# Three edits to a joined kernel: order of the values in the local attention, transposes in pairs of 64 rows in the causal attention, and a diagonal term in pairs of 64 rows in the last attention

## The reference

```
layer 0, ffn branch: 6 x { local attention (16 heads of 64, windows of 32, each looks at
                           itself and the window before), then a gated feed-forward }
layer 2, attn branch: sim = (q k^T)/8 + slope_h * (j - i), masked to j <= i; softmax; @ v
                      (16 heads of 64)
layer 3, attn branch: logits = (q k^T)/sqrt(8) - alpha_h * |i - j|; softmax; @ v
                      (16 heads of 8, no mask)
```

## Time and profile before

| what | value |
|---|---|
| median of 3 runs | 4435.03 us (4434.4 to 4439.9) |
| the profiled execution, its own time | 4430.25 us |
| its span | 4428.5 us |
| TensorE (PE), weight loads (PEld) | 3915.2 us (88%), 2158.4 us (49%) |
| VectorE, ScalarE, GpSimd | 3103.5 (70%), 2556.6 (58%), 1247.7 us (28%) |
| granted clock of TensorE, mean | 0.926 |

### The profile page before, as it was taken

One profiled execution on the slowest core, in us unless ns is written; L12 is line 12 of the kernel. 1 busy time (PEld: TensorE's weight loads), 2 busy tenths in 40 slices (PEclk: granted clock), 3 DMA queues, 4 the chain that ended last, 5 costly groups with the idle time before them and its releaser, 6 DMA issues.

```text
span 4428.5 us, 113349 instructions
## 1 busy us (share of the span) xinstructions
PE 3915.2 (88%) x46366; PEld 2158.4 (49%) x46462; DVE 3103.5 (70%) x5185; ACT 2556.6 (58%) x3768; POOL 1247.7 (28%) x1082
## 2 busy tenths in 40 slices
PE   3789999999999999867778999999997599999997
PEld 1365555555555555535553555555553233333333
DVE  7788888888888888645414666666664677777772
ACT  5456666666666667552224555555553276767774
POOL 0366656655566566310000000000000011111220
PEclk7899999999999999965578999999998699999998
DMA  0222222222222222201000000000000300000000
GB/s 18 71 67 75 69 65 80 71 72 74 65 76 72 68 76 68 55 10 24 21 9 17 3 4 4 4 2 4 4 1 26 100 19 20 19 20 19 19 2 15
DMA packets 85355, 166.74 MB, mean 38 GB/s; under 512 B 23336, under 2 KB 37336, under 8 KB 83568
## 3 DMA queue, kind: packets, MB, share of 16 engines
q1 hardware_dynamic: 84816, 159.13, 13.8%
HBM read 40.60 MB, written 8.52 MB: 11 GB/s over the span
## 4 chain that ended last, share of the span: by engine, by line
PE 46%; issue 19%; POOL 15%; DVE 12%; ACT 5%; DMA 1%; SPq 1%; POOLq 0%; DVEq 0%; ACTq 0%
POOL arena L987 7%; POOL arena L991 6%; PE banks L1287 6%; PE banks L2237 5%; PE banks L1270 4%; PE banks L1258 4%; ACT arena L2373 2%; PE banks L522 2%; PE banks L2195 2%; PE banks L2211 2%; PE banks L1306 1%; DVE arena L861 1%; DVE arena L1438 1%; PE banks L2215 1%; PE banks L605 1%
## 5 line engine op out<-in xcount | busy, mean ns | idle before, releaser
L2447 DVE TENSOR_REDUCE arena<-banks 128x2 f32<-128x1024 f32 x512 | 614.2, 1223 | 248.6 <-PE banks L2202 140.4
L2373 ACT ACTIVATE arena<-banks 128x1024 f32<-128x1024 f32 x512 | 522.8, 1025 | 252.7 <-PE banks L2218 134.2
L987 POOL TENSOR_TENSOR arena<-arena 128x512 f32<-128x512 f32 x384 | 424.5, 1127 | 637.4 <-DVE arena L870 629.8
L991 POOL TENSOR_TENSOR arena<-arena 128x1024 f32<-128x1024 f32 x192 | 533.1, 2776 | 15.1
L1438 DVE CUSTOM_DVE_ANT_0 arena<-arena,banks 128x512 f32<-128x512 f32 (+3 forms) x640 | 361.9, 603 | 202.6 <-issue 201.3
L1381 ACT ACTIVATE arena<-banks 128x512 f32<-128x512 f32 (+3 forms) x320 | 170.2, 532 | 401.7 <-PE banks L1270 401.0
L522 PE MATMUL banks<-arena 128*128 128x512 f32 x768 | 366.7, 622 | 30.8 <-issue 15.0
L2237 PE MATMUL banks<-arena 128*32 128x256 f32 x4096 | 334.4, 393 | 14.2 <-issue 8.7
L1518 POOL COPY arena<-arena 128x512 f32<-128x512 f32 x32 | 19.6, 613 | 1123.5 <-DVE arena L1464 1123.5
L1373 ACT ACTIVATE arena<-arena 128x128 f32<-128x128 f32 (+15 forms) x256 | 328.6, 1285 | 11.3 <-DVE arena L1450 6.3
L1258 PE MATMUL banks<-arena 64*128 64x512 f32 (+3 forms) x1280 | 322.3, 581 | 5.1 <-issue 3.8
(11 more groups left out here) (433 smaller groups left out, 7384.3 us busy)
## 6 DMA issues: line engine op xcount, KB each, us to landing
arena<-arena SPq DMA_DIRECT2D x768, 64.0 KB
arena<-arena SPq DMA_DIRECT2D x96, 384.0 KB, 3.6
arena<-arena SPq DMA_DIRECT2D x96, 128.0 KB, 3.4
arena<-in_lf_wqkv SPq DMA_DIRECT2D x6, 1024.0 KB, 6.0
arena<-features_k SPq DMA_DIRECT2D x32, 128.0 KB
arena<-arena SPq DMA_DIRECT2D x8, 512.0 KB
arena<-features_q SPq DMA_DIRECT2D x16, 216.0 KB
arena<-in_lf_wqkv SPq DMA_DIRECT2D x6, 512.0 KB, 3.8
```

Source lines behind the costliest of these rows:

```text
L987: nc.gpsimd.tensor_tensor(r[:, :, e * H2:(e + 1) * H2], q[:, j, :, (1 - e) * H2:(2 - e) * H2], s[:, j, 1, e * H2:(e + 1) * H2].unsqueeze(1 ...
L991: nc.gpsimd.tensor_tensor(a, a, lf_rb, ALU.add).then_inc(S("lf_rot" + x), 1)
L2373: nc.scalar.activation(bi_PT[n % 4], PS[:, 2 * bi_slot("S", n):2 * bi_slot("S", n) + 2].rearrange("p a b -> p (a b)"), ACT.Exp).then_inc(S ...
L2447: nc.vector.tensor_reduce(bi_max[j % 2][:, t, :, c], PS[:, 2 * slot:2 * slot + 2], AX.X, ALU.max).then_inc(S("bi_mx"), 1)
```

## The change

It does three things. In the local attention, `values` is one call that does both parities before `project`. In the causal attention, each 128 x 128 transpose becomes two of 64 rows: the lower rows of both heads go to bank 4, the upper rows to bank 5; VectorE and ScalarE evict the same number of elements as before, now for both heads each; `turn` waits for both copies first, and carries markers (`sem_inc`). In the last attention, each matmul of the diagonal term is cut by its contraction into 64-row halves, with the slope of head 0 on rows 0 to 63 and of head 1 on rows 64 to 127, so that the two heads' matmuls stand side by side.

```diff
 (local attention)
-            def values(n, l, e):
-                vb = (lf_Vs if e == 0 else lf_V)[n % 4]
-                for p in range(8):
...
-                if e:
-                    m.then_inc(S("lf_pv"), 1)
+            def values(n, l):
+                for e, vb in enumerate((lf_Vs[n % 4], lf_V[n % 4])):
+                    for p in range(8):
...
+                m.then_inc(S("lf_pv"), 1)
 (its step)
                 if lf_live(s - 3, end):
-                    values(s - 3, l, 0)
+                    values(s - 3, l)
                 if lf_live(s - 4, end):
                     project(s - 4, l, end)
                 if ffn and j == 0:
                     var(c, l)
-                if lf_live(s - 3, end):
-                    values(s - 3, l, 1)
 (causal attention)
+                n = min(4, at_row(c, x) + 1 - 4 * b)
+                if i >= 1:
+                    pe.wait_ge(S("at_ptA"), l * 80 + i)
+                    pe.wait_ge(S("at_ptB"), l * 80 + i)
                 for h in range(2):
                     if b == 0:
                         pe.wait_ge(S("at_exp"), l * 64 + (2 * (2 * c + x) + h + 1))
-                    if i >= 1:
-                        pe.wait_ge(S("at_ptB" if h else "at_ptA"), l * 80 + i)
-                    for j in range(min(4, at_row(c, x) + 1 - 4 * b)):
-                        m = nc.tensor.transpose(PS[:, 4 + h, j * P:(j + 1) * P], ck(at_E[c % 2][x][h], 4 * b + j, P), ident)
-                    m.then_inc(S("at_trB" if h else "at_trA"), 1)
+                        pe.sem_inc(S("at_turning"), 1)
+                    elif h == 0:
+                        pe.sem_inc(S("at_turning"), 1)
+                    for j in range(n):
+                        k = h * n + j
+                        lower = nc.tensor.transpose(PS[:, 4, k * at_D:(k + 1) * at_D], ck(at_E[c % 2][x][h], 4 * b + j, P)[0:at_D], ident[0:at_D, 0:at_D])
+                        upper = nc.tensor.transpose(PS[:, 5, k * at_D:(k + 1) * at_D], ck(at_E[c % 2][x][h], 4 * b + j, P)[at_D:P], ident[at_D:P, at_D:P])
+                lower.then_inc(S("at_trA"), 1)
+                upper.then_inc(S("at_trB"), 1)
 (VectorE's copy; ScalarE's takes the upper 64 columns from bank 5 likewise)
-                nc.vector.tensor_copy(at_PT[x][0][:, 4 * b:4 * b + n, t % 2 * P:(t % 2 + 1) * P],
-                                      PS[:, 4, 0:n * P].rearrange("p (a b) -> p a b", b=P)).then_inc(S("at_ptA"), 1)
+                nc.vector.tensor_copy(at_PT[x][:, :, 4 * b:4 * b + n, t % 2 * P:t % 2 * P + at_D],
+                                      PS[:, 4, 0:n * P].rearrange("p (h a b) -> p h a b", h=2, b=at_D)).then_inc(S("at_ptA"), 1)
 (last attention; scores likewise)
-                    for h in range(2):
-                        for x in range(3):
-                            m = nc.tensor.matmul(PS[:, 2 * slot + h, t * P:n], ck(bi_aI[p], 2 * x + h, P), bi_trib[:, 0:P], start=False, stop=x == 2)
+                    for y in range(6):
+                        for h in range(2):
+                            m = nc.tensor.matmul(PS[:, 2 * slot + h, t * P:n], ck(bi_aI[p], y, P)[rows(h)], ck(bi_trib, y % 2, P)[rows(h)], start=False, stop=y == 5)
 (VectorE, once)
+            for h in range(2):
+                r = slice(64 * h, 64 * h + 64)
+                st(nc.vector.tensor_copy(bi_slope[r, :, 8:11], bi_slope[r, :, 0:6].rearrange("p a (x h) -> p a x h", h=2)[:, :, :, h]))
 (GpSimd, for each pair of heads)
-                for x in range(6):
-                    m = nc.gpsimd.tensor_tensor(ck(bi_aI[p], x, P), ident, bi_a[p][:, x:x + 1].broadcast_to([P, P]), ALU.mult)
+                for y in range(6):
+                    m = nc.gpsimd.tensor_tensor(ck(bi_aI[p], y, P), ck(bi_tri, 4 + y % 2, P), bi_a[p][:, 8 + y // 2:9 + y // 2].broadcast_to([P, P]), ALU.mult)
```

More of the change, by code:

```diff
@@ L1166, in program @@
         at_E = [[[arena.f32(n) for _ in range(2)] for n in (T // 2, T)] for _ in range(2)]
-        at_PT = [[arena.f32_3(n, 2 * P) for _ in range(2)] for n in (NB // 2, NB)]
+        at_PT = [arena.f32(2 * n * 2 * P).rearrange("p (h k q) -> p h k q", h=2, k=n) for n in (NB // 2, NB)]
         at_mx = [arena.f32_3(2, 4) for _ in range(2)]
@@ L2033, in program @@
         bi_cut = arena.bf16(bi_H)
[L2034 to L2037, removed]
+        bi_slope = arena.f32_3(8, 11)
+        bi_a = [arena.f32(11) for _ in range(2)]
+        bi_tri = arena.f32(6 * P)
+        bi_trib = arena.bf16(4 * P)
         bi_aI = [arena.bf16(6 * P) for _ in range(2)]
@@ L2212, in scores @@
                 if k // 4 == G:
-                    for h in range(2):
-                        for x in range(3):
-                            m = nc.tensor.matmul(PS[:, 2 * slot + h, n:n + P], ck(bi_aI[p], 2 * x + h, P), bi_trib[:, P:2 * P], start=False, stop=x == 2)
+                    for y in range(6):
+                        for h in range(2):
+                            m = nc.tensor.matmul(PS[:, 2 * slot + h, n:n + P], ck(bi_aI[p], y, P)[rows(h)], ck(bi_trib, 2 + y % 2, P)[rows(h)], start=False, stop=y == 5)
                 if n:
@@ L2336, in bi_act @@
             nc.scalar.activation(bi_idb, ident, ACT.Copy).then_inc(S("bi_idb"), 1)
-            nc.scalar.activation(bi_trib, bi_tri, ACT.Copy).then_inc(S("bi_idb"), 1)
+            nc.scalar.activation(bi_trib, bi_tri[:, 0:4 * P], ACT.Copy).then_inc(S("bi_idb"), 1)
             for c in range(NCH):
@@ L2738, in layout @@
     p = np.arange(P)
-    o["at3_tri"] = np.concatenate([-2 * np.maximum(p[None] - p[:, None], 0), -2 * np.maximum(p[:, None] - p[None], 0)], 1).astype(np.float32)
+    half = [p % 64 + 64 * f for f in range(2)]
+    o["at3_tri"] = np.concatenate([-2 * np.maximum(p[None] - x[:, None], 0) for x in half] + [-2 * np.maximum(x[:, None] - p[None], 0) for x in half]
+                                  + [p[None] == x[:, None] for x in half], 1).astype(np.float32)
     off = (p[:, None, None] + 128 * np.arange(4) - 512 * np.array([[1], [0]]))[:, :, None, :, None] * np.array([-1, 1])[None, None, :, None, None]
```

17 lines of the change are left out of this document (8 added, 9 removed).

## The result

The changed kernel takes 4365.3 us (median of four runs, 4359.6 to 4377.1) against 4434.7 for the kernel before on the same chip: ratio 0.9847, 95% interval 0.9823 to 0.9871. That is 69 us less where 128 were forecast, and 5 us above the top of the range given (4360). The profiled execution has a span of 4366.3 us, 62 less than before.

What follows compares the result with a forecast made beforehand. TensorE was taken to set the time in the causal and last attention, until VectorE is met. Terms -80 - 44 + 2 - 6 = -128 took 4430.25 to 4302, as a median 4307 us; range 4272 to 4360.

Steps and rivals of the forecast that it cites:

- Rivals B: Weight loads don't go under matmuls of their own rows, so a pair takes 0.114 us: 4374 us; chance 0.08.
- C: Causal transposes: the two halves don't run at once, each costing what a whole one does: 4596 us; chance 0.03.
- part 1: Causal attention's transposes as 64-row pairs: TensorE's sequence 130 us shorter, of which -80 us is kept; ends -125 and +209.
- the forecast's 0.5 and 0.6: Causal attention: TensorE's wait for copies, some 0.5 us in an odd pass and 0.6 in an even pass's last two units.
- the unit with the addition: Causal odd pass: after VectorE's addition L1477 the turn waits for two logits, a copy and the addition, 2.6 us, mostly covered.
- rival A: Causal attention: VectorE or ScalarE takes the gain; only even passes gain, 42 us instead of 80, so 4345; chance 0.13.
- Part 2: Last attention's diagonal matmuls as 64-row pairs: 472 changes of rows at 0.1 us go, -44 us; ends -50 and +88.
- Part 3: Local attention with both parities' values before project: two changes of rows fewer, -6 us; ends -32 and +15.
- ordinary ones: Local attention: two of every four steps were to gain 0.33 us each, from two changes of rows fewer.
- the one ahead of the variance: Local attention: the step before the variance gains only 0.17 us, as ScalarE's L762 waits there for VectorE's chain.
- the fourth: Local attention: every fourth step loses 0.55 us, as the variance starts later and delays ScalarE's copy and qk's second half.
- Rival D: Local attention: each fourth step costs 1.5 us instead of 0.55, 23 us more, so 4330; chance 0.06.

Runs made afterwards that it cites:

- -33 alone: The kernel before with the change of the causal attention alone (pairs of 64-row transposes): 4401.0 us, ratio 0.9926.
- the one with the forty instructions: The changed kernel with 40 semaphore instructions more on TensorE at the start of each pass of the local attention's loop: 4398.9 us in one execution.
- -34 alone: The kernel before with the change of the last attention alone (diagonal matmuls in pairs of 64 rows): 4399.8 us, ratio 0.9925.

## Why the prediction was wrong

- **What bounds the kernel; prices.** Right. A pair costs 0.063 us (0.06 forecast), the twelve matmuls 0.34 (0.35), the change of rows before them falls away (0.16 became 0.07), and one kind of even pass can lose 2.06 (2.1). Rivals B and C are out by the first timeline. The Trainium skill (TensorE: Matmul & The Clock Gate, Part 3) lets loads overlap between different row groups, and the trace agrees for these halves: L1274's load starts at 2643.96 with the matmul of L1273.
- **How much of part 1 stays: the step that failed.** "TensorE needs 10.7 there afterwards ... all but some 0.5: the pass goes to 11.2". Odd passes were forecast to lose 1.2 us in the mean; they lose 0.25 where the clock stays up (13.29, 12.79, 13.26 and 13.11 become 13.29, 12.37, 12.93 and 12.85) and 0.04 with the clock's losses counted. Even ones lose 1.3 of the 1.5 forecast. The wait for the copies is 58.5 us, not the 35 that the forecast's 0.5 and 0.6 make over 32 passes each. I counted that wait once per pass, from the unit with the addition. It comes in every unit in which TensorE has only scores and a turn, about 1.5 us of work now, while VectorE needs 1.8 by its starts (0.61 each, from 2642.08 to 2643.30 above) or 2.05 by its lengths for two logits and a whole copy. This is rival A (-42; measured -36, and -33 alone), with its mechanism in the form of a chain, not of a full engine. The prediction's own sign of being wrong had this too: a causal window above 930 us with L1457 (now L1462) ahead of the turn. It came out at 941.
- **The clock.** Part 1 was summed at 1.00. With the stage's idle time up from 14 to 69 us it was 0.98, in one profile 0.97: 9.5 us in six passes and 5 at the stage's end. One profile of the same causal code (the one with the forty instructions) has no pass at half clock between the first and the last few, and its stage takes 932.4 us. Nothing in the profile of before shows it for this stage.
- **Part 2.** Right in place and size (-41.9 in the full profile; -34 alone, where waits at the loop's start took back the rest).
- **Part 3.** The steps named were right: 0.4 off ordinary ones (0.33 forecast), nothing for the one ahead of the variance (0.17), 0.6 more for the fourth (0.55). Rival D's 1.5 is out. What failed is that the run of 64-row blocks was costed by its matmuls alone. It has 256 instructions in 1.9 us, and their code doesn't always arrive in time: 18 us of breaks, 3 more before L621, then half clock, against 6 us gained at the loop's end (15.0 to 8.8). The Trainium skill (Runtime: NRT & Kernel Launch, Instruction fetch mechanics) says that code comes in blocks of 16 KiB, 256 instructions, and that crossing into the next is mostly hidden. The trace agrees with the size (420 packets, 6.88 MB). It agrees with "mostly hidden" for most of the 96 runs of values, and not for the 13 places where one breaks off.
- **The sum.** -3 + 17 (local), -36, -42, +1 make -63, against -62 in the span. The range gave part 3 no way to lose more than 15 us, and no chance was given to rival A and a loss in part 3 together; both came.

Open: when TensorE asks for its next piece of code; whether less traffic of the other DMA queue would shorten the long breaks, as the packets' times suggest (no run varies it); what the markers in each turn cost (no run takes them away).

## What to carry to other kernels

When one engine's part of a unit gets shorter, cost each unit of the loop by itself: the gain ends where the chain through the other engines (here scores, two logits, copy, turn) is longer than the engine's own work, though its total has slack. Count instructions as well as columns: a run of hundreds of tiny matmuls needs its code as fast as it uses it, so look in the trace for idle time put down to "issue" inside one line's run, and for what the DMA queues carry just before it. Of two orders with the same changes of rows, try both, since here project ahead of the values is 30 us better than behind them.

## What the hardware showed that was not expected

- TensorE can run out of code in a run of 256 instructions in 1.9 us: at a few fixed instructions of the program, not in every pass, for 0.7 to 3.9 us, and 40 instructions more in front move the place by 40. One packet of 16 KiB lands 1.2 to 1.6 us before the engine goes on. The breaks of over 3 us all had some 5 us of dense other DMA traffic (share 0.80 to 0.86) in front of their packet.
- Forty semaphore instructions in a row on TensorE cost 0.14 to 0.15 us each when nothing covers them (33.5 and 35.9 us for 240).
- Two 64-row fp32 transposes on different halves of the array take 0.063 us together; a 128-row one takes 0.108.
- Short idle times can cost twice: half clock for 3.4 us or more came after each break of over 3 us, and in four odd passes of one kind right behind waits of 0.9 and 0.6 us. Three passes of the same kind kept the full clock with the same waits.
